# Splitting the exponential of the windowed attention into one instruction per head

## What is computed

```python
sim = jnp.einsum('bhwid,bhwjd->bhwij', bq, bk)
mask = (i < j) | (i > j + WINDOW) | (j == -1)
sim = jnp.where(mask, -jnp.finfo(sim.dtype).max, sim)
attn = jax.nn.softmax(sim, axis=-1)
out = jnp.einsum('bhwij,bhwjd->bhwid', attn, bv)
```

## Time and profile before

| what | value |
|---|---|
| median of 3 timed runs | 4763.89 us (4763.55 to 4797.42) |
| the profiled execution's own time | 4583.2 us |
| its span on the slowest core (core 0) | 4581.3 us |
| spans of the 8 cores | 4565.0 to 4581.3 us |
| mean granted TensorE clock of the cores | 0.717 to 0.721 |
| busy share: TensorE, VectorE, ScalarE, GpSimd | 67%, 33%, 22%, 7% |

### The profile page before, as it was taken

How to read it: one execution, slowest core, us unless ns; L and a number is a source line. 1 busy time by engine, 2 the same in 40 slices (tenths; PEclk the granted TensorE clock), 3 DMA queues, 4 the chain that set the end, 5 groups by cost and what they waited for, 6 DMA issues and landing times.

```text
span 4581.3 us, 43056 instructions; the slowest of 8 cores (4565.0 to 4581.3 us)
## 1 busy us (share of the span) xinstructions
PE 3090.9 (67%) x11353; PEld 1069.0 (23%) x11488; DVE 1514.5 (33%) x3019; ACT 1018.1 (22%) x1209; POOL 340.0 (7%) x433
## 2 busy tenths in 40 slices
PE   3646566676626667777579599466677775885795
PEld 1212121121102222222134144122222221331341
DVE  1322322212224444444511421344444444124313
ACT  0022425445301222222111120112222221111111
POOL 0000000000012300000010010222000000100010
PEclk9866777787767755555689699677555566886896
DMA  4110000000040010000142041200000011422232
GB/s 116 21 16 1 0 0 1 1 0 1 1 119 19 1 24 1 1 1 10 22 74 47 1 74 18 43 19 14 10 1 1 1 24 27 67 45 62 46 59 58
DMA packets 52862, 119.54 MB, mean 26 GB/s; under 512 B 5884, under 2 KB 6140, under 8 KB 50576
## 3 DMA queue, kind: packets, MB, share of 16 engines
q0 software_dynamic: 43120, 82.93, 11.3%
q1 hardware_dynamic: 9504, 33.85, 2.2%
HBM read 174.07 MB, written 16.78 MB: 42 GB/s over the span
## 4 chain that ended last, share of the span: by engine, by line
PE 52%; DVE 16%; ACT 14%; issue 10%; DMA 7%; DVEq 1%; ACTq 0%; POOLq 0%; POOL 0%; another core or an unknown queue 0%; SPq 0%
PE PS L1414 6%; PE PS L1383 6%; PE PS L1374 6%; ACT AR L1103 5%; PE PS L863 3%; PE PS L1005 3%; ACT AR L588 3%; PE PS L606 3%; PE PS L560 3%; DMA AR<-fqkv 2%; PE PS L654 2%; PE PS L1094 2%; PE PS L917 2%; DVE AR L1113 1%; PE PS L1080 1%
## 5 line engine op out<-in xcount | busy, mean ns | idle before, releaser
L1383 PE MATMUL PS<-AR 128*128 128x512 bf16 (+1 forms) x1408 | 555.4, 394 | 52.6 <-DVE AR L1356 49.5
L1374 PE MATMUL PS<-AR 128*128 128x512 bf16 (+1 forms) x1352 | 533.9, 395 | 77.5 <-DVE AR L1397 61.4
L1103 ACT ACTIVATE AR<-PS 128x1024 bf16<-128x1024 f32 x224 | 229.4, 1024 | 742.5 <-PE PS L1094 533.7
L588 ACT ACTIVATE AR<-PS 128x1024 bf16<-128x1024 f32 x320 | 310.1, 1021 | 318.6 <-PE PS L560 200.8
L1397 DVE SCALAR_TENSOR_TENSOR AR<-PS,FBIA,AR 128x512 bf16<-128x512 f32 (+1 forms) x176 | 132.1, 751 | 584.7 <-PE PS L1383 383.0
L1414 PE MATMUL PS<-AR 128*128 128x512 bf16 (+1 forms) x1377 | 318.7, 383 | 8.4 <-ACT AR L1390 4.3
L1136 PE MATMUL PS<-AR 128*65 128x512 bf16 x448 | 234.2, 625 | 100.7 <-DVE AR L1119 78.6
L560 PE MATMUL PS<-AR 64*128 64x512 bf16 x640 | 200.3, 491 | 134.8 <-ACT AR L588 87.4
L863 PE MATMUL PS<-AR 128*128 128x512 bf16 x499 | 160.3, 488 | 142.6 <-DMA AR<-fqkv 116.1
L1390 ACT ACTIVATE AR<-PS,FBIA 128x512 bf16<-128x512 f32 (+1 forms) x176 | 120.9, 687 | 563.5 <-PE PS L1383 410.6
L606 PE MATMUL PS<-AR 128*65 128x512 bf16 x640 | 213.4, 458 | 46.1 <-DVE AR L593 46.1
(11 more groups left out here) (162 smaller groups left out, 3350.4 us busy)
## 6 DMA issues: line engine op xcount, KB each, us to landing
AR<-fw1p POOLq DMA_DIRECT2D x176, 256.0 KB, 3.6
AR<-fw POOLq DMA_DIRECT2D x42, 256.0 KB, 4.0
XT<-xt SPq DMA_DIRECT2D x8, 1024.0 KB, 22.0
xin_spill<-XT SPq DMA_DIRECT2D x8, 1024.0 KB, 16.7
AR<-rot SPq DMA_DIRECT2D x16, 512.0 KB, 4.3
XT<-xin_spill POOLq DMA_DIRECT2D x32, 256.0 KB, 4.2
out_xt<-XT SPq DMA_DIRECT2D x32, 256.0 KB, 2.2
AR<-fqkv POOLq DMA_DIRECT2D x16, 384.0 KB, 4.7
```

What stands on the lines that cost most here:

```text
L588: return eng.activation(out=pt[:, 0:1024], in_=bank(sb, 0, 1024), func=AF.Exp)
L1103: return eng.activation(out=pt[:, 0:1024], in_=bank(2, 0, 1024), func=AF.Exp)
L1374: return eng.matmul(out=bank(ch, 0, 512, 0, hcs), lhsT=w[:, 0:hcs], rhs=h2n_t(dc)[:, ch * 512:(ch + 1) * 512], start=(dc == 0), stop=(dc = ...
L1383: return eng.matmul(out=bank(2 + ch, 0, 512, 0, hcs), lhsT=w[:, 0:hcs], rhs=h2n_t(dc)[:, ch * 512:(ch + 1) * 512], start=(dc == 0), stop=( ...
```

## The change

The exponential over both banks becomes two exponentials, one per side, each 128x512. The mask and the memset of a side are emitted right behind that side's exponential. The probability buffer's key becomes a key per side, and the value product of a side reads the key of its own side. Every one of these operations still writes `r_tail`. What is computed is the same, and no matmul, mask, memset or DMA is added or removed; in TensorE's list the order is the same.

```diff
-    PTFK = ["f2pt0", "f2pt1"]
+    PTFK = [("f2pt0a", "f2pt0b"), ("f2pt1a", "f2pt1b")]
...
-
-            def ex(eng, pt=pt):
-                return eng.activation(out=pt[:, 0:1024], in_=bank(2, 0, 1024),
-                                      func=AF.Exp)
-            B.emit("S", ex, reads=("ps2", "ps3"), writes=(ptk, "r_tail"),
-                   tag=f"{L}s2e.{hp}.{w}.{tj}")
             for side in range(2):
+                def ex(eng, pt=pt, side=side):
+                    return eng.activation(out=pt[:, side * 512:(side + 1) * 512],
+                                          in_=bank(2 + side, 0, 512), func=AF.Exp)
+                B.emit("S", ex, reads=(f"ps{2 + side}",),
+                       writes=(ptk[side], "r_tail"),
+                       tag=f"{L}s2e.{hp}.{w}.{tj}.{side}")
                 for (r, mk) in masks:
...
-                    B.emit("V", vmask, reads=(ptk,) + CR, writes=(ptk, "r_tail"),
+                    B.emit("V", vmask, reads=(ptk[side],) + CR,
+                           writes=(ptk[side], "r_tail"),
                            tag=f"{L}s2vm.{hp}.{w}.{tj}.{side}.{r}")
-            for side in range(2):
                 if ka > 0:
                     B.emit("V", lambda eng, pt=pt, side=side, ka=ka: eng.memset(
                         pt[:, side * 512:side * 512 + ka * 128], 0.0),
-                        writes=(ptk, "r_tail"), tag=f"{L}pz0.{hp}.{w}.{tj}.{side}")
+                        writes=(ptk[side], "r_tail"), tag=f"{L}pz0.{hp}.{w}.{tj}.{side}")
...
-                B.emit("T", pv, reads=(f"fv.{tj}", ptk, "r_v"), writes=(f"ps{nb}",),
-                       tag=f"{L}pv.{h}.{w}.{tj}")
+                B.emit("T", pv, reads=(f"fv.{tj}", ptk[side], "r_v"),
+                       writes=(f"ps{nb}",), tag=f"{L}pv.{h}.{w}.{tj}")
```

More of the change, by code:

```diff
@@ L1124, in s2stage @@
                         pt[:, side * 512 + (kb + 1) * 128:side * 512 + 512], 0.0),
-                        writes=(ptk, "r_tail"), tag=f"{L}pz1.{hp}.{w}.{tj}.{side}")
+                        writes=(ptk[side], "r_tail"), tag=f"{L}pz1.{hp}.{w}.{tj}.{side}")
         def s2pv(tj):
```

## The result

The changed kernel is slower: its time is 1.018 times that of the kernel before, with a 95% interval of 1.0125 to 1.0234. The medians are 4690.23 us (4638.83 to 4846.41, 10 runs) against 4645.74 us (4572.35 to 4797.42, 10 runs). These medians mix undisturbed runs with runs in which the cores of a die had a lower granted clock, while the ratio uses undisturbed runs alone; that is also why the kernel before has another median here than in its table above. The profiled execution took 4670.74 us, its slowest core 4668.8 us. Compared again in a later set, the same kernel gave 1.0128 (1.0081 to 1.0175).

The account below looks back on a forecast made before the run. The attention stretches were taken as a latency chain, the slower of a VectorE and a TensorE loop setting each step. Large pairs at +2.22 us gave 53, small ones 5, together +59 on the median: 4823 us, range 4793 to 4870.

Parts of the forecast that it names:

- The half's price: Each 128x512 exponential from PSUM on ScalarE was taken to cost 0.60 us, two costing 1.20 instead of 1.02.
- the hop to the held exponential: Time from VectorE's end of side 0's work to the second exponential's start, taken as 0.10 us, bounds 0.08 and 0.32.
- VectorE's loop: Second exponential's end through mask 1 and memset 1 to the next first exponential: 0.65 + m us, m being gap and memset.
- my TensorE loop: Second exponential's end through score matmul and side 0's n selections to the next first exponential: 0.97 + 0.105 n us.
- The lone score matmul: Second score matmul on TensorE, no longer overlapped by the first, was to cost the full 0.54 us before the selections.
- the rival of a cheaper matmul: Lone score matmul takes 0.27 us less in TensorE's loop: +32 us, 4796 us; cases below +48 us had chance 0.21.
- "Net 0": Interval -1 to 0: next pair's scores start 0.42 us later, but the exponential needs four selections less, -0.42.
- the cover I named for VectorE: Reductions queued behind mask 1 start over 3 us after the exponential, covering mask 1's lateness; otherwise 0.3 us a pair.
- "overlap wins": Rival: the second exponential is not held by VectorE and starts 0.60 us after the first; 4668 us, chance 0.07.
- Dearer halves: Rival: exponential of 0.687 us adds 35 us, hop of 0.32 adds 44, both give 4902; over +80 us, chance 0.20.

Follow-up runs that it names:

- the dummy memset: Changed kernel plus one 128-column VectorE memset per step behind side 0's mask and memset, writing unread scratch and r_tail; 1.0279 to the kernel before.
- the free key: Changed kernel with r_tail read instead of written by the windowed attention's exponentials, masks and memsets; 0.9709 to the kernel before, median 4470.07 us.
- the order of emission: Changed kernel, same keys, with both exponentials emitted ahead of the masks and memsets; 0.9991 to the kernel before.
- The kernel with both halves ahead of the masks: Kernel before with its exponential divided into two 128x512 ahead of the masks, whole-buffer key and r_tail still written; 1.0038 to the kernel before.
- the shortened reductions: Last stabilizer reduction of each side cut to 128 columns; large pair 40.51 us in the changed kernel, 38.75 in the kernel before, one execution each.

## Why the prediction was right and where it was wrong

The forecast of the difference held. It was +59 us, +1.2% to +1.3%; the stretches grew by 58 us, the compared runs by 1.8% (1.25% to 2.34%) and 1.28% (0.81% to 1.75%). It was slower, as forecast with 0.72. The mechanism was the one described, and the dummy memset, the free key and the order of emission each confirm it separately.

The step that failed is the one that puts the difference on a base: "The median is 181 us above that execution, and the attention stage already runs at the lower clock, so I add the same 59 us to the median: 4823 us". The median of the changed kernel is 4690, outside 4793 to 4870. The three timed runs that I built on were all long ones of this kernel; with ten runs its median is 4646, 118 us lower. The profiled execution at 4583 stood in the table beside them and near the lowest of all ten, 4572. The same 59 us put on 4646 would have been 4705. The other figure of the same sum, 4642 for an execution like the profiled one, held: core 0 of the changed kernel took 4637.6, and the profiled execution of the second comparison 4643.3. I had seen a gap of 181 us, three times the effect, and left it out of the range. How such gaps can arise the row of core 2 above shows, 31 us by the feed-forward stage at another clock; what made the three timed runs long stays open, as neither a trace nor a clock of them is on record. The range of a time needs the spread of the base as well as that of the difference.

The steps of a large pair, measured against the forecast (core 2's timeline above, and the earlier trace rows):

| interval | before | forecast | after |
|---|---|---|---|
| -4 to -3 | 3.07 | 3.42 | 3.36 |
| -3 to -2 | 2.92 | 3.385 | 3.33 |
| -2 to -1 | 2.84 | 3.36 | 3.30 |
| -1 to 0 | 10.57 | 10.57 | 10.58 |
| 0 to 1 | 2.63 | 2.925 | 3.28 |
| 1 to 2 | 2.65 | 3.15 | 3.09 |
| 2 to 3 | 2.92 | 3.21 | 3.11 |
| 3 to the logarithm | 4.14 | 4.05 | 3.98 |
| whole pair | 38.76 | 40.98 | 40.95 |

- The half's price, 0.60, was right (597 ns), and so was the hop to the held exponential, 0.10: it is 0.09 (1917.23 to 1917.32), at the low end of the bounds. But it was right by luck, since I had counted the waits wrong. By the rule of `finalize` the exponential of position -2 has five waits, not three: first VectorE, then the two value products of two steps before, then the last selection of each side. The one of position -3 has three, not two. So it is two waits more that cost 0.12, and each costs 0.06, not 0.11. What counts is how many stand behind the one that blocks: four gives 0.32, two 0.20, and none, as in the held exponential, 0.09. The kernel with both halves ahead of the masks has one such wait at position -3 and three at -2, and fits between them, with 0.14 (1869.04 to 1869.18) and 0.26 (1872.05 to 1872.31), core 0; the changed kernel in another order has one and two, and takes 0.14 and 0.20.

```profile
1868.66 0.38 DVE L1125 MEMSET AR<- 128x384 bf16 x1 [0.22 <-DVE AR L1125]
1869.18 1.28 ACT L1104 ACTIVATE AR<-PS 128x512 bf16<-128x512 f32 x2 [2.00 <-DVE AR L1125]
...
1871.78 0.27 DVE L1125 MEMSET AR<- 128x256 bf16 x1 [0.19 <-DVE AR L1125]
1872.31 1.29 ACT L1104 ACTIVATE AR<-PS 128x512 bf16<-128x512 f32 x2 [1.84 <-DVE AR L1125]
```

- Position 2 to 3 was forecast as VectorE's loop with a hop of 0.31. In the changed kernel a first exponential has three waits at most, VectorE's first, so that hop is 0.20 by the same measure, and the trace names TensorE there (the row at 1945.75). With 0.20 my TensorE loop would have set this interval at 3.175; the rest is the small shortfall of the other intervals.
- The waits of ScalarE for memsets before the change were in 56 of the 112 steps, not 32: the earlier trace rows shows L1119 alone, and the view has another row, below, for L1123. ScalarE stood idle there for 104.4 us in all, not 56.7. The sum doesn't suffer, since it was built step by step from the timeline.

```profile
ACT AR L1103 <- DVE AR L1123: 47.7, 24, 2.3
```

- The lone score matmul costs nearly its full length: from 1918.06 to the selections at 1918.57, 0.51 where I took 0.54. The Trainium skill (TensorEngine Tiling (Array Packing), Key Properties) says that a change of tiling mode drains the engine. The trace is in line with it, as the selections start only near the end of the matmul of 0.58, but no run here tells a drain from the matmul's own length. It was no half, so the rival of a cheaper matmul falls. Most intervals came out 0.05 to 0.07 short of the forecast, half of it from here.
- "Net 0" for -1 to 0 was right, but the cover I named for VectorE was not looked at on its other side. I checked that the reductions would not be delayed by mask 1 and missed that mask 0 of the next step would be delayed by the reductions. Before, the first exponential after the scores ended at 1921.60, 0.2 us after the last reduction (at 1921.38, first row below), and the masks followed at once:

```profile
1918.12 3.26 DVE L1032 TENSOR_REDUCE AR<-PS 128x1 f32<-128x640 f32 x4 [0.30 <-PE PS L1019]
...
1921.71 0.56 DVE L1113 TENSOR_TENSOR AR<-AR,CSTB 128x128 bf16<-128x128 bf16 x2 [0.33 <-ACT AR L1103]
```

Now it starts 0.42 earlier relative to them and is half as long, so it ends at 1936.87, the reductions at 1937.48, and mask 0 starts at 1937.40 as they end, 0.53 late instead of 0.11. That makes up the 0.36 by which 0 to 1 was missed, and the shortened reductions give it back (0.44 in the pair), in the changed kernel only. The pair's sum, 40.98 for 40.95, is that near by luck: this error and the six intervals that are short, by 0.40 in all, cancel.
- The rival "overlap wins" was the right picture of the kernel without the key: I had it at 4668 us on the median of then, -96 us, -2.0%, and the version with the free key took -2.9%. It decided at the point named, the wait of the second exponential on VectorE.
- Dearer halves: neither bound came true. What makes L1390 cost 687 ns where the half costs 597, its Gelu or its bias column, no run shows. The hop of 0.32 belongs to four waits behind the one that blocks.

Not settled: why the first comparison gave 1.018 and the second 1.013. Their intervals overlap, and 56 to 58 us of 4581 is 1.2% to 1.3%; the clock on single cores may account for the rest, but no experiment showed that.

## What to carry to other kernels

Before an operation is split so that its halves overlap with something, list every key that each half writes and reads, also those that stand for a whole region: one shared key turned an intended overlap into a relay between two engines, and cost +1.3%, where the same division without it gives -2.9% (1.2% of that is the key's own, without any division). If the key can't be removed, emit all producers first and their followers after: here that took the loss back (0.9991), but gave no gain. And when work is moved earlier in relation to a queue on another engine, look at what was in that queue on both sides, ahead of the moved work and behind it.

## What the runs showed of the hardware

Two exponentials of 597 ns that follow each other without a wait take 1.08 us together, 0.11 less than their sum; with a wait of the second on the first they take 1.28 to 1.29, 0.09 more. The prediction took 1.20 for the overlap rival. The Trainium skill (ScalarE: Activation LUTs, What ACT_TABLE_LOAD costs) states an overlap of about 93 ns for ACTIVATEs back to back; the trace has 0.11, and it is lost where the second waits for the first's semaphore.

From the end of a VectorE operation to the start of the exponential that it releases pass 0.09 us when that wait is the exponential's last, and 0.14, 0.20, 0.26 and 0.32 when one, two, three and four more waits stand behind it, although those are met already: some 0.06 us for each. It is not their number alone that counts: of two waits, VectorE's costs 0.14 when it is the first and 0.09 when it is the last. By these rows, putting the wait that ends last behind the others would be worth up to 0.23 us in a step of the kernel before that a memset sets; this was not tried.
